# A transformer block in split arithmetic: the part after the heads rewritten in f16, token-major and with its chunks interleaved

## The reference

```python
x = x + attn_a(layernorm(x), Wq, Wk, Wv, bq, bk, bv, Wo, bo)   # causal, 16 heads of 64, times Wo (1024x128)
x = x + ffn(layernorm(x), w1, b1, w2, b2)                      # relu(x @ w1 + b1) @ w2 + b2, width 512
x = x + attn_b(layernorm(x), W_qk, W_v, alibi_slope)           # causal, one head of 128, scores + (kpos - qpos) * slope
x = x + ffn(layernorm(x), w1, b1, w2, b2)                      # the same weights again
```

## Time and profile before

| | us |
|---|---|
| median of 3 runs (lowest, highest) | 599.29 (599.08, 599.47) |
| the profiled execution | 598.35 |
| its span, first to last instruction | 596.6 |
| PE busy | 550.6 (92%) |
| DVE busy | 468.8 (79%) |
| ACT busy | 458.6 (77%) |
| POOL busy | 400.9 (67%) |
| mean granted PE clock | 0.973 of 2.4 GHz |

### The profile page before, as it was taken

The page is one execution under the profiler, slowest core; times in us unless marked ns, Lnnn a source line. Parts: engine busy times, 40 slices in busy tenths (PEclk is TensorE's granted clock), DMA queues, the critical chain, the costliest instruction groups (busy, mean ns, idle before and its releaser), DMA issues.

```text
span 596.6 us, 16752 instructions
## 1 busy us (share of the span) xinstructions
PE 550.6 (92%) x6314; PEld 392.8 (66%) x6314; DVE 468.8 (79%) x1440; ACT 458.6 (77%) x877; POOL 400.9 (67%) x382
## 2 busy tenths in 40 slices
PE   4788999899999999999999999989799998789796
PEld 3454666566666766676667667656688776657674
DVE  4578888788888888888888888873378798688674
ACT  3668889889899989998998999889355883264485
POOL 5669899778888888888888888889500231066310
PEclk9989999999999999999999999999899997799799
DMA  8622323233342432333333424304571000000001
GB/s 194 159 54 66 88 82 106 55 90 91 91 107 59 113 98 74 106 92 90 91 84 92 112 55 116 88 31 169 194 240 44 1 1 0 1 1 1 2 19 53
DMA packets 35328, 47.89 MB, mean 80 GB/s; under 512 B 10776, under 2 KB 16688, under 8 KB 35248
## 3 DMA queue, kind: packets, MB, share of 16 engines
q1 hardware_dynamic: 33136, 46.29, 28.7%
q10 hardware_dynamic: 2112, 0.54, 0.5%
HBM read 12.21 MB, written 9.44 MB: 36 GB/s over the span
## 4 chain that ended last, share of the span: by engine, by line
PE 68%; DVE 12%; issue 9%; ACT 8%; POOL 2%; DMA 1%; SPq 0%; DVEq 0%; ACTq 0%; POOLq 0%
PE psum L531 9%; PE psum L587 8%; PE psum L588 8%; PE psum L485 7%; PE psum L487 6%; PE psum L486 6%; PE psum L569 5%; PE psum L567 5%; PE psum L568 5%; PE psum L743 2%; PE psum L590 2%; ACT p L1007 2%; DMA w_raw<-in_L_attn_a_Wk 1%; DVE st_lo L1144 1%; ACT p_hl L1008 1%
## 5 line engine op out<-in xcount | busy, mean ns | idle before, releaser
L1577 POOL TENSOR_TENSOR p_hl<-p,p_hl 128x512 f16<-128x512 f32 x288 | 326.2, 1158 | 46.9 <-ACT p_hl L1008 43.4
L1161 DVE CUSTOM_DVE_ANT_0 max_junk<-psum,mask_s 128x1024 bf16<-128x1024 f32 (+7 forms) x256 | 190.2, 753 | 32.6 <-issue 32.4
L1007 ACT ACTIVATE p<-psum 128x512 f32<-128x512 f32 x288 | 177.0, 615 | 17.1 <-PE psum L590 14.1
L1008 ACT ACTIVATE p_hl<-psum 128x512 f16<-128x512 f32 x288 | 178.1, 618 | 0.0
L567 PE MATMUL psum<-v_all,p_hl 128*128 128x65 f16 x1152 | 125.9, 194 | 2.8 <-POOL p_hl L1577 2.8
L568 PE MATMUL psum<-v_all,p_hl 128*128 128x64 f16 x1152 | 126.0, 193 | 0.0
L587 PE MATMUL psum<-q_hl,k_hh 128*128 128x512 f16 (+3 forms) x384 | 125.4, 327 | 0.5 <-ACT p_hl L1008 0.4
L569 PE MATMUL psum<-v_all,p_hl 128*128 128x65 f16 x1152 | 125.5, 195 | 0.0
L588 PE MATMUL psum<-q_hm,k_l 128*128 128x512 f16 (+3 forms) x384 | 122.1, 327 | 0.0
L567 PEld LDWEIGHTS psum<-v_all,p_hl 128*128 128x128 f16 x1152 | 107.9, 98 | 17.7 <-POOL p_hl L1577 3.0
L568 PEld LDWEIGHTS psum<-v_all,p_hl 128*128 128x128 f16 x1152 | 107.1, 98 | 4.8
(11 more groups left out here) (189 smaller groups left out, 1091.4 us busy)
## 6 DMA issues: line engine op xcount, KB each, us to landing
k_hh<-st_hi SPq DMA_DIRECT2D x64, 128.0 KB, 2.3
o_scratch<-o_sb SPq DMA_DIRECT2D x16, 512.0 KB, 2.6
o_in<-o_scratch SPq DMA_DIRECT2D x4, 2048.0 KB, 8.8
k_l<-st_lo SPq DMA_DIRECT2D x32, 128.0 KB, 2.4
q_hl<-st_hi SPq DMA_DIRECT2D x32, 128.0 KB, 2.3
q_hl<-st_lo SPq DMA_DIRECT2D x32, 128.0 KB, 2.4
q_hm<-st_hi SPq DMA_DIRECT2D x32, 128.0 KB, 2.4
x_sb<-in_L_attn_a_x SPq DMA_DIRECT2D x4, 256.0 KB, 3.8
```

The lines of the kernel that those rows point to most:

```text
L1007: nc.scalar.activation(p32[:, ring_at(u, r), :], src, ACT.Exp, scale=SCALE_A).then_inc(exp_done, 1)
L1008: nc.scalar.activation(p_hl[:, u % 2, 0, BANK * r:BANK * (r + 1)], src, ACT.Exp, scale=SCALE_A).then_inc(phi_done, 1)
L1161: nc.vector.tensor_tensor_reduce(out=max_junk[:, n % 2, 0:cols], in0=max_banks(v, j, 0, cols), in1=mask_s[:, S - cols:S], scale=1.0, scala ...
L1577: nc.gpsimd.tensor_tensor(p_hl[:, u % 2, 1, cols], p32[:, ring_at(u, r), :], p_hl[:, u % 2, 0, cols], ALU.subtract)\
```

## The change

Everything ahead of the last head slots stays as it is, but for loads and weight preparation; the tail is new.

**f16.** Wo, w1, w2, W_qk and W_v are scaled by a power of two each, found from their norms, and split into f16 halves; `oT`, `xT`, `h` and `qb` are f16 too. The casts of Wo, w1 and w2 leave the start; they are loaded again after the projections of the heads are over, ACT takes squares of six weights in slot 30 (`tail_squares`), PE sums them ahead of slot 31, and ACT and DVE split them among the last exponentials (`tail_high`, `tail_low`).

**Token-major.** In the projection and in the second product of the feed-forward the tokens are stationary and 128 columns of the weight move, so that the result is token-major: `yT`, its ACT pass and `turn_result` are gone, and DVE adds two tiles of 128 tokens at a time to `x_sb` (`add_result(k, half)`), with the scale. The biases bo and b2 are added to `x_sb` ahead by POOL (`add_output_row`, `add_forward_row`).

**Normalisation.** `xn` is written by ACT (`late_norm`), for which POOL also makes `-mean*rstd`.

**Interleaving.** The tail is a written list of calls for each engine; chunks of different layers follow each other, and the first 9 blocks of `o_in` are turned between the last head's products. The first `o_in` chunks are fetched in slots 28 and 29 in place of 30 and the end.

**Low halves of h.** Of the first feed-forward DVE subtracts them, of the second POOL.

```diff
+            def output_tile(c, j):
...
+                rows, cols = slice(P * j, P * (j + 1)), slice(P * (j % 2), P * (j % 2) + P)
+                for blk in range(OB):
+                    last = three(bank(Y_BANKS[0][j // 2])[:, cols], oT_hi[:, c % 2, blk, rows], oT_lo[:, c % 2, blk, rows], wo_hi[:, blk, :], wo_lo[:, blk, :],
+                                 start=(blk == 0), stop=(blk == OB - 1))
+            def hidden(y, m):
...
+                three(bank(H_BANKS[n % 2]), w1_hi[:, blk], w1_lo[:, blk], xT_hi[:, cols], xT_lo[:, cols]).then_inc(h_full, 1)
+            def forward(y, j):
+                if j == 0:
+                    pe.wait_ge(h_lo_done[y // CHUNKS], FW * (y % CHUNKS + 1))
...
+                for m in range(FW):
+                    r = (FW * y + m) % H_RING
+                    last = three(bank(Y_BANKS[1 + y // CHUNKS][j // 2])[:, cols], h_hi[:, r, rows], h_lo[:, r, rows], w2_hi[:, m, :], w2_lo[:, m, :],
+                                 start=(m == 0), stop=(m == FW - 1))
@@ scalar
+            def hidden_high(y, m):
...
+                if n >= H32_RING:
+                    act.wait_ge(h_lo_done[(n - H32_RING) // (FW * CHUNKS)], (n - H32_RING) % (FW * CHUNKS) + 1)
@@ vector
-            def output_b(b, j):
+            def outputs_out_b(b, j):
...
+                nc.vector.tensor_scalar(ob_den[:, m % 2:m % 2 + 1], src[:, E:V2W], tail_gains[:, 4:5], None, ALU.mult).then_inc(ob_scaled, 1)
+                nc.vector.reciprocal(ob_inv[:, m % 2:m % 2 + 1], ob_den[:, m % 2:m % 2 + 1]).then_inc(ob_inverse, 1)
+                nc.vector.scalar_tensor_tensor(out=x_sb[:, m, :], in0=src[:, 0:E], scalar=ob_inv[:, m % 2:m % 2 + 1],
+                                               in1=x_sb[:, m, :], op0=ALU.mult, op1=ALU.add).then_inc(ob_read, 1)
@@ gpsimd
+            def hidden_low(y, m):
+                n = FW * y + m
+                pool.wait_ge(h32_done, n + 1)
+                pool.wait_ge(h_hi_done, n + 1)
+                nc.gpsimd.tensor_tensor(h_lo[:, n % H_RING, :], h32[:, n % H32_RING, :], h_hi[:, n % H_RING, :], ALU.subtract)
+            def late_rstd(n):
+                chunk_rstd(n)
+                chunk_shift(n)
```

More of the change, by code:

```diff
@@ L107, in hybrid_block @@
     ST_RING = 3
[L108 to L109 removed]
+    S_RING = 3
+    H32_RING = 3
     GH = 4
@@ new lines, in _ @@
+            queries_b(0)
+            turn_late(ln_of[2, 1])
+            hidden(2, 0)
+            hidden(2, 1)
+            values_b(0)
+            hidden(2, 2)
+            hidden(2, 3)
+            queries_b(1)
+            turn_late(ln_of[1, 3])
+            max_tile_b(0, 0)
+            values_b(1)
+            max_tile_b(0, 1)
+            hidden(3, 0)
+            forward(2, 0)
+            hidden(3, 1)
+            max_tile_b(0, 2)
+            hidden(3, 2)
+            forward(2, 1)
@@ new lines, in _ @@
+            turn_late(ln_of[3, 2])
+            forward(4, 1)
+            hidden(5, 3)
+            forward(4, 2)
+            hidden(6, 0)
+            forward(4, 3)
+            hidden(6, 1)
+            turn_late(ln_of[3, 3])
+            hidden(6, 2)
+            forward(5, 0)
+            hidden(6, 3)
+            forward(5, 1)
+            forward(5, 2)
+            forward(5, 3)
+            hidden(7, 0)
+            hidden(7, 1)
+            hidden(7, 2)
+            forward(6, 0)
+            hidden(7, 3)
@@ L913, in _ @@
+            forward(6, 1)
+            forward(6, 2)
+            forward(6, 3)
+            forward(7, 0)
+            forward(7, 1)
+            forward(7, 2)
+            forward(7, 3)
         @block.scalar
@@ L1581, in _ @@
+            for u in range(HEADS - 1):
                 for r in range(NU):
@@ L1623, in _ @@
-            for c in range(1, CHUNKS):
-                chunk_rstd(3 * CHUNKS + c)
+            tail_root()
+            low(HEADS - 1, 0)
+            low(HEADS - 1, 1)
+            low(HEADS - 1, 2)
+            low(HEADS - 1, 3)
+            low(HEADS - 1, 4)
+            add_output_row(0)
+            low(HEADS - 1, 5)
+            low(HEADS - 1, 6)
+            low(HEADS - 1, 7)
+            low(HEADS - 1, 8)
+            late_rstd(ln_of[1, 0])
+            add_output_row(1)
+            steps_begin()
@@ new lines, in _ @@
+            add_forward_row(3)
+            late_rstd(ln_of[2, 2])
+            late_rstd(ln_of[2, 3])
+            low_b(0, 0)
+            low_b(0, 1)
+            low_b(0, 2)
+            low_b(0, 3)
+            low_b(0, 4)
+            low_b(0, 5)
+            low_b(0, 6)
+            low_b(0, 7)
+            low_b(0, 8)
+            late_rstd(ln_of[3, 0])
+            low_b(1, 0)
+            add_forward_row(4)
+            low_b(1, 1)
+            low_b(1, 2)
+            low_b(1, 3)
+            low_b(1, 4)
```

1341 lines of the change are left out of this document (878 added, 463 removed).

## The result

The changed kernel took 578.57 us (median of 4 runs, 577.84 to 579.24), and the kernel before, with the runs beside it, 599.18 (596.79 to 599.47). The ratio is 0.9664 with a 95% interval of 0.9637 to 0.9692: 3.4% faster. The forecast was 570 (555 to 588), so way and range held, and the size was 28 us where 21 came. A second run of the same kernel, used as the base of the experiments, gave 0.9655 (0.9631 to 0.9680).

A forecast was written before the change was run, and what follows sets the result against it. PE, busy for 92% of the span, was taken as the bound: heads' end 425.7 + PE's work 117.8 + waits 22.5 + 0.5 + 2.75 = 569.3, with 1.75 outside the span 571.0, put at 570 us; range 555 to 588.

The forecast's parts named there:

- PE's sum: PE's work in the tail behind the heads' end: 117.8 us, 15 less than the 133 counted before.
- 36 us of waits: Waits and half clock in the tail before the change; the rest of any gain must come from them.
- rival D: No change beyond measurement: the tail's old waits return in full, 584.6 by its sum; chance 0.01.
- The heads' end: End of the last head: 1.3 us later, 425.7 instead of 424.4, with POOL's last low halves covering ACT's added passes.
- The waits: PE's waits and half clock in the tail after the change: 22.5 us in all.
- The chains: Chunks crossing layers in the tail: 3 us for the first two crossings, 0.5 each for the other ten.
- The 4 for POOL's sixteen low halves: Second feed-forward: POOL ends its low halves of h later than PE needs them, 4 us of waits.
- the score banks: Second attention: score banks four deep between PE, DVE and ACT, 3 us of waits.
- The half clock: PE's speed lost to a lowered clock in the tail: 2.5 us, against 10 before.
- A: Tail: the interleaving hides almost every wait, leaving waits of 10, 558 us; chance 0.16.
- B: Late stages of the tail: POOL and its meetings with DVE set the pace, 582 us; chance 0.23.
- C: Tail: written lists can't overtake, so each of 12 chains is exposed, 611 us at 4 each; chance 0.05.

The follow-up runs named there:

- e_no_rows: Changed kernel with POOL's twelve passes that add bo and b2 left out, a small memset in place of each: 576.86 us, ratio 0.9647 to the kernel before.
- e_layered: Changed kernel with the same operations but the layers one behind the other again on each engine: 600.53 us, ratio 1.0053 to the kernel before.
- e_slopes_act: Changed kernel with the two multiplications of the bias tiles by the slope moved from POOL to ACT: 579.73 us, ratio 0.9710 to the kernel before.

## Why the prediction was right, and where it missed

**PE's sum** held: 117.8 against 117.5, at a pitch of 0.055 to 0.057. Its step to "15 less than before" was 2 too small, because the kernel before does 134.9 and not 133: I counted 72 score products as f16 of 512 columns (15.8), and there are 96, with the 24 that add a row, float32r, half of them 512 wide and the rest narrower (17.6). That error enters the 36 us of waits, and so rival D, but not the forecast. One row was misread as well: the 0.50 at 479.57 is one product with its way through the array and not two; the pitch of 0.23 is right all the same.

**The heads' end** was the step that failed most for its size: 1.3 forecast, 3.9 measured (5.0 against the mark), and 428.3 is outside the 424.4 to 427 that I had named as the sign of being right. I took POOL's last low halves as cover for ACT's passes. They were no cover for the squares, because POOL needs the exponentials behind them: it stood 3.43 for one. And POOL's own run had grown by some 3.4, with the gains, the first row and a low half stretched by DVE's pass, none of which I had priced on the path. I had also not priced `tail_diagonal`, one small DVE pass, which with the squares costs 2.1.

**The waits** were 22.5 forecast, and 28.0 and 26.6 in two executions. The chains were about right (8 forecast for all, 6.3 of stands on `xn`, some 7.5 as losses). The 4 for POOL's sixteen low halves was wrong in kind: PE waits 0.6 for them, and with them on DVE nothing changes. The maxima of both sequences are 2.8 of stands, for 5 forecast on the second; the score banks, 3 forecast, show as no stand and 0.6 of losses. In their place stand waits that I had not listed: 2.7 for the relu's second pass, 1.8 for one low half at 496.6, 1.3 for blocks of `o_in`, and some twenty losses of 0.15 to 0.55. The half clock cost 3.4 (0.05 of 20 and 0.12 of 20) for my 2.5; its 0.88 breaks the sign "no stage below a clock of 0.9".

**Where the gain came from.** I wrote that the gain beyond PE's work must come from the 36 us of waits. It came mostly from PE's work: the losses went only from 33.2 to 28.0. But the experiments show that this reading misleads. With shorter PE work and the layers in order, the losses are 51.3 and nothing is gained, or 42.1 and some 5 us gained with w1 and w2 alternating as before; the interleaving takes 14 to 24 of them away. In both of these orders PE's shorter work turned for the most part into waits, and the mixing of layers filled them.

**The rivals.** A (waits of 10) did not happen. B (582) has the time nearest to what came, with a total 3.4 below it. Its sign came too, DVE passes of 1 and more beside POOL (1.15, 1.21, 1.46), but it is not shown to be the cause in the tail: taking POOL's side of the meetings away in e_no_rows gave nothing. Ahead of the heads' end such meetings did cost, in the diagonal and in POOL's stretched low half. That the sum of waits came within 6 is in part luck: the 4 for POOL's low halves and the 3 for the score banks, which hardly came, made up for waits that I had not listed. C did not happen in the changed kernel, and e_layered, whose time is at C's bound, has not its mechanism: only 1.3 of its waits are for `xn`, the rest for relu passes, maxima, low halves and one transfer. What C says of written lists, a 1/sqrt stuck behind something else on POOL, is seen once, in e_slopes_act.

## What to carry to other kernels

In this tail of dependent stages a cut of 17 us of PE's work gave between nothing and some 5 us until the order was rewritten as well, in the two orders that were tried. In such a case price both together, and check the waits that the shorter work leaves open; here about the old sum of waits remained. Before an engine's run is called the cover of another's added work, follow what feeds that run, and count what the change adds to the run itself. Small costs on different engines ahead of one wait must be removed together, and a one-at-a-time trial can call both free.

## What the runs showed that was not expected

- Taking 3.8 us of work off ACT left the heads' end no earlier: the clock granted to PE was 0.66 in the next 5 us behind a stand of 1.5; with that stand gone too it was 1.00.
- A DVE pass over 128 columns can last as long as POOL's pass beside it: 1.21 for one at 397.04, and 2.48 for two that took 0.65 elsewhere. It goes the other way too: a POOL pass of 1.15 took 2.13 beside DVE's low half of Wo.
- POOL's multiplication of a 128x1024 tile by a column took 2.86 and 3.30 us, against 1.04 for an affine_select of the same size. Taking them off POOL gained nothing.
- One and the same program reaches the mark at 82.17 or 83.83 us: of the 3.3 us between two of its executions (spans of 573.5 and 576.8) half is made before the work of this change begins, and 1.4 in the tail.
